# Graph message passing on one core: a round's superblock numbers are loaded into registers once instead of five times

## What is computed

```python
h = jnp.maximum(_layernorm(x, axis=-1), 0.0)
xs = h[src]
for i in range(4):
    msgs = msgs + jnp.where((edge_type == i)[:, None], xs @ W[i] + b[i], 0.0)
out = x + jax.ops.segment_sum(msgs, dst, num_segments=12500)
```

## Time and profile before

| | us |
|---|---|
| median of 3 runs | 2284.09 |
| lowest and highest run | 2275.62, 2289.59 |
| the profiled execution | 2289.54 |
| its span, first to last instruction | 2287.8 |
| POOL busy | 1477.3 (65%) |
| PE busy | 1023.3 (45%) |
| DVE busy | 672.9 (29%) |
| ACT busy | 149.9 (7%) |

### The profile page before, as it was taken

One profiled execution on the slowest core, in us unless ns is written; L12 is line 12 of the kernel. 1 busy time (PEld: TensorE's weight loads), 2 busy tenths in 40 slices (PEclk: granted clock), 3 DMA queues, 4 the chain that ended last, 5 costly groups with the idle time before them and its releaser, 6 DMA issues.

```text
span 2287.8 us, 18293 instructions
## 1 busy us (share of the span) xinstructions
PE 1023.3 (45%) x4086; PEld 704.6 (31%) x4087; DVE 672.9 (29%) x1535; ACT 149.9 (7%) x399; POOL 1477.3 (65%) x1573
## 2 busy tenths in 40 slices
PE   5774243334444444444444444444444444443234
PEld 2232233223232323232323232333233333233234
DVE  5554123133232323232323232323232323121123
ACT  3341000000000000000000000000000000000000
POOL 6666666656666666666666666666666666666663
PEclk9886566666666666666666666666666566655566
DMA  8663111111111111111111111111111111111241
GB/s 249 220 206 111 45 46 44 48 37 45 47 45 47 45 47 45 47 45 47 45 47 45 47 45 47 45 48 45 47 45 46 45 47 45 47 45 45 69 116 43
DMA packets 95392, 144.22 MB, mean 63 GB/s; under 512 B 27481, under 2 KB 57683, under 8 KB 95363
## 3 DMA queue, kind: packets, MB, share of 16 engines
q0 software_dynamic: 50016, 102.50, 17.1%
q1 hardware_dynamic: 40567, 38.92, 5.2%
q10 hardware_dynamic: 4780, 2.51, 0.4%
HBM read 111.73 MB, written 32.09 MB: 63 GB/s over the span
## 4 chain that ended last, share of the span: by engine, by line
POOL 40%; issue 28%; PE 13%; another core or an unknown queue 12%; DVE 3%; DVEq 2%; DMA 1%; ACT 0%; SPq 0%; ACTq 0%; POOLq 0%
POOL messages L367 32%; POOL lists L367 8%; PE ps_sum L815 6%; PE ps_y L773 3%; PE ps_y L839 2%; DVE lists L641 1%; PE ps_y L832 0%; DVE stage L553 0%; PE ps_sum L764 0%; DVEq L661 0%; DVE acc L632 0%; DVE stats L493 0%; DMA lists<-in_dst 0%; DVE ps_node L670 0%
## 5 line engine op out<-in xcount | busy, mean ns | idle before, releaser
L367 POOL DMA_INDIRECT messages<-message_table,table_row x1155 | 1090.0, 944 | 559.5 <-issue 336.1
L815 PE MATMUL ps_sum<-messages,lists 128*128 128x128 f32 x1776 | 353.7, 334 | 440.5 <-issue 407.4
L815 PEld LDWEIGHTS ps_sum<-messages,lists 128*128 128x128 f32 x1776 | 298.3, 238 | 480.9 <-issue 479.3
L632 DVE SCALAR_TENSOR_TENSOR acc<-ps_sum,own_tile,acc x203 | 70.4, 347 | 1112.9 <-remote 1037.6
L367 POOL DMA_INDIRECT lists<-message_table,table_row x288 | 271.8, 944 | 154.2 <-issue 83.0
L815 PE MATMUL ps_sum<-messages,onehot 128*128 128x128 f32 x582 | 132.1, 363 | 274.0 <-issue 256.6
L641 DVE SCALAR_TENSOR_TENSOR lists<-ps_node,node_iota,dst_col 128x1024 f32<-128x1024 f32 x148 | 190.0, 1284 | 114.4 <-issue 55.9
L815 PEld LDWEIGHTS ps_sum<-messages,onehot 128*128 128x128 f32 x582 | 114.8, 269 | 302.3 <-issue 302.2
L815 PE MATMUL ps_sum<-lists 128*128 128x128 f32 x592 | 127.3, 358 | 143.3 <-issue 132.1
L839 PE MATMUL ps_y<-stage 128*128 128x512 f32 x136 | 116.9, 896 | 146.5 <-issue 111.4
L353 POOL DMA_INDIRECT early_x<-in_x,src_col x119 | 112.6, 946 | 65.8 <-issue 33.0
(11 more groups left out here) (89 smaller groups left out, 580.6 us busy)
## 6 DMA issues: line engine op xcount, KB each, us to landing
message_table<-stage SPq DMA_DIRECT2D x98, 256.0 KB
messages<-message_table,table_row POOLq DMA_INDIRECT x1155
out<-acc SPq DMA_DIRECT2D x24, 256.0 KB
lists<-message_table,table_row POOLq DMA_INDIRECT x288
acc<-in_x SPq DMA_DIRECT2D x4, 896.0 KB
early_x<-in_x,src_col POOLq DMA_INDIRECT x119
acc<-in_x ACTq DMA_DIRECT2D x2, 896.0 KB, 5.8
acc<-in_x SPq DMA_DIRECT2D x1, 832.0 KB
```

The lines of the kernel that those rows point to most:

```text
L367: pool.indirect_dma_start(messages[k][0:rows, t, :], None, table_rows, bass.IndirectOffsetOnAxis(ap=flat_rows[0:rows, at + t:at + t + 1], ...
L632: ins = nc.vector.scalar_tensor_tensor(out=rows, in0=sums, scalar=mine[:, bass.ds(place, 1)], in1=rows, op0=ALU.mult, op1=ALU.add)
L815: ins = nc.tensor.matmul(ps_sum[:, bass.ds(q % BANKS, 1), 0:d], onehots[k][:, t, :], messages[k][:, t, :], start=(t == 0), stop=(t == tile ...
```

## The change

VectorE no longer loads its four numbers at each superblock. At the head of a round it loads the 20 numbers of the five superblocks at once into 20 registers, and each superblock copies three of them to the registers it counts with. TensorE gets a row of its own that holds nothing but counts (`windows_row`) and loads the five counts of a round at once into five registers. The early superblocks and the last one keep a load of their own (VectorE with the new function, TensorE's early ones with the old). The new row needs one more VectorE instruction, one more DMA on SP, and all who waited for `ranges_ready` at 16 now wait for 32. POOL's program stays as it is. The diff, cut to its core:

```diff
+    windows_row = sb("windows_row", [1, chunks, sb_per_chunk], I32)
+    windows_by_chunk = sb("windows_by_chunk", [chunks, sb_per_chunk], I32)
...
-            sp.wait_ge(ranges_made, 1)
+            sp.wait_ge(ranges_made, 2)
             sp.dma_start(ranges[:, :, :], ranges_by_chunk[:, :, :].rearrange("c s k -> c (s k)")).then_inc(ranges_ready, 16)
+            sp.dma_start(windows_row[:, :, :], windows_by_chunk[:, :]).then_inc(ranges_ready, 16)
...
             dve.wait_ge(own_steps, 8)
+            nc.vector.tensor_scalar_add(windows_by_chunk[:, :], ranges_by_chunk[:, :, 3], 0.0).then_inc(ranges_made, 1)
...
-            def superblock(s, home, tiles, keys=0):
-                windows_reg = dve.alloc_register(f"dve_windows_{nc.next_id()}")
-                dve.reg_load([at_reg, place_reg, tile_reg, windows_reg], flat_ranges[0:1, bass.ds(s * 4, 4)])
+            def load_round(s, sbs):
+                dve.reg_load([reg for regs in round_regs[0:sbs] for reg in regs], flat_ranges[0:1, bass.ds(s * 4, sbs * 4)])
+
+            def superblock(s, k, home, tiles, keys=0):
+                first_at, first_place, first_tile, windows_reg = round_regs[k]
+                dve.reg_mov(at_reg, first_at)
+                dve.reg_mov(place_reg, first_place)
+                dve.reg_mov(tile_reg, first_tile)
...
                 for m in range(EARLY_ROUNDS * SLOTS):
-                    superblock(s + m, onehots[m % SLOTS], SB_TILES)
+                    if m % SLOTS == 0:
+                        load_round(s + m, SLOTS)
+                    superblock(s + m, m % SLOTS, onehots[m % SLOTS], SB_TILES)
...
-                superblock(i, early_onehot, SB_TILES, keys)
+                load_round(i, 1)
+                superblock(i, 0, early_onehot, SB_TILES, keys)
...
-            def superblock(s, k, tiles, needed, release_slot=True):
-                windows, regs = load_windows(pe, s)
+            def load_round(s, sbs):
+                pe.reg_load(window_regs[0:sbs], flat_windows[0:1, bass.ds(s, sbs)])
+
+            def superblock(k, tiles, needed, release_slot=True):
+                windows = pe.snap(window_regs[k], min_val=1, max_val=node_tiles)
...
             def table_round(i):
+                load_round(i * SLOTS + EARLY_SBS, SLOTS)
                 for k in range(SLOTS):
-                    superblock(EARLY_SBS + i * SLOTS + k, k, SB_TILES, (i + 1) * (16 * SB_TILES))
+                    superblock(k, SB_TILES, (i + 1) * (16 * SB_TILES))
```

More of the change, by code:

```diff
@@ L243, in gnn_program @@
     flat_ranges = ranges[:, :, :].rearrange("p c s -> p (c s)")
+    flat_windows = windows_row[:, :, :].rearrange("p c s -> p (c s)")
     flat_rows = table_row[:, :, :].rearrange("p c t -> p (c t)")
@@ L432, in _ @@
             act.wait_ge(stage_free, 1)
-            act.wait_ge(ranges_ready, 16)
+            act.wait_ge(ranges_ready, 32)
             pair_reg, pair = counter(act, "early_pair")
@@ L591, in _ @@
             dve.wait_ge(own_steps, 10)
-            dve.wait_ge(ranges_ready, 16)
+            dve.wait_ge(ranges_ready, 32)
             for k in range(Y_SLOTS):
@@ L657, in next_pair @@
                 dve.reg_add(pair_reg, pair_reg, 1)
-            def superblock(s, home, tiles, keys=0):
-                windows_reg = dve.alloc_register(f"dve_windows_{nc.next_id()}")
-                dve.reg_load([at_reg, place_reg, tile_reg, windows_reg], flat_ranges[0:1, bass.ds(s * 4, 4)])
+            round_regs = [[dve.alloc_register(f"dve_{name}_{k}") for name in ("at", "place", "tile", "windows")] for k in range(SLOTS)]
+            def load_round(s, sbs):
[5 more added lines that the diff above has]
+                dve.reg_mov(tile_reg, first_tile)
                 windows = dve.snap(windows_reg, min_val=1, max_val=node_tiles)
@@ L750, in _ @@
             table_rounds(rounds - LATE_ROUNDS, rounds)
-            superblock(full_sbs, onehots[0], last_tiles)
+            load_round(full_sbs, 1)
+            superblock(full_sbs, 0, onehots[0], last_tiles)
             settled_windows()
@@ L799, in _ @@
             pe.wait_ge(loaded_b, 16)
-            pe.wait_ge(ranges_ready, 16)
+            pe.wait_ge(ranges_ready, 32)
             pe.wait_ge(y_ready, node_tiles + 2)
@@ L805, in _ @@
             p_reg, early_count = counter(pe, "early_pair")
-            def superblock(s, k, tiles, needed, release_slot=True):
-                windows, regs = load_windows(pe, s)
+            window_regs = [pe.alloc_register(f"pe_windows_{k}") for k in range(SLOTS)]
+            def load_round(s, sbs):
+                pe.reg_load(window_regs[0:sbs], flat_windows[0:1, bass.ds(s, sbs)])
+            def superblock(k, tiles, needed, release_slot=True):
+                windows = pe.snap(window_regs[k], min_val=1, max_val=node_tiles)
                 with pe.Fori(0, windows):
@@ L866, in _ @@
                 table_round(i)
-            superblock(full_sbs, 0, last_tiles, rounds * 16 * SB_TILES + 16 * last_tiles, False)
+            load_round(full_sbs, 1)
+            superblock(0, last_tiles, rounds * 16 * SB_TILES + 16 * last_tiles, False)
 _INS = ["x", "src", "dst", "edge_type_4", "L0_gnn_W", "L0_gnn_b"]
```

6 lines of the change are left out of this document (2 added, 4 removed).

## The result

The change made the kernel slower: median 2354.26 us (2347.84 to 2357.37, four runs) against 2286.84 us for the kernel before (2275.62 to 2304.51, four runs) on the same chip; ratio 1.0284, 95% interval 1.0213 to 1.0355. The profiled execution has a span of 2354.9 us at a granted clock of 0.636, before it was 2287.8.

A forecast was written before the change was run, and what follows sets the result against it. POOL's gathers, 1.420 us each with pauses, were taken as the bound; the parts summed to -0.3 + 0 + 0 + 0 - 1.7 = -2 us, so 2282 us for the median, range 2267 to 2293.

The forecast's parts named there:

- What bounds: POOL's 1443 gathers at 1.420 us, pauses included, take 2049 of 2068 us; some 19 us are waits for others.
- Part 1: 144 loads fewer on TensorE and VectorE each, not on the path in the rounds; 0.3 us gained at the end.
- Part 2: Bigger loads at a round's head, 0.63 us on VectorE and 0.36 on TensorE, hidden: 0, range 0 to +0.9 us.
- Part 3: VectorE's register copies, 69 ns each, replace an address piece of that size: nothing.
- Part 4: Second row's instruction and DMA delay the rounds' start at most 1.1 us, hidden behind the gather: 0, range 0 to +1.
- Part 5: POOL's waits behind early superblocks: marks slightly earlier, three short holes go, 1.7 us gained, of 0 to 30 us.
- Rival B: Mark behind an early superblock misses the quick stretch, POOL stops 17.2 us; two more stops give 2318 us; chance 0.07.
- Rival A: TensorE late by its sequencer in slow stretches; fewer instructions remove all POOL's mark waits, 30 us, giving 2254; chance 0.09.
- C: Count row delays the start, all waiting for two DMAs; 12 us DMA to be seen, 35 for 1%; chance 0.01.
- D: Change doesn't do what it says: a load of 20 at 5 x 344 ns eats the saving, 2284 us, inside the forecast.

The follow-up runs named there:

- h5: Kernel before with both long loads added at each round's head, every short load kept, on a chip with pauses: 2294.54 us, ratio 1.0012.
- e2: Kernel before with VectorE's part alone (one load of twenty per round, register copies), no second row: 2299.39 us, ratio 1.0005.
- e3: Kernel before with only the row of counts and its DMA added, read by nobody, all loads as before: 2300.4 us, ratio 0.9993.
- h1: The change unaltered, repeated on a chip with pauses, against the kernel before: 2370.69 us, ratio 1.0291.
- h2: The change with TensorE's load of five cut into four and one, on a chip with pauses: 2379.72 us, ratio 1.0375 to before.
- e4: The change with both engines' loads cut to at most four registers, on a chip with pauses: 2302.48 us, ratio 1.001 to before.
- f1: The change unaltered on a chip without pauses, against the kernel before: 0.36% faster.
- f5: Kernel before with both long loads added and all short loads kept, on a chip without pauses: the added loads cost nothing.
- g1: The change unaltered, run again on a chip without pauses, against the kernel before: 0.3% faster.
- g5: Kernel before with both long loads added and short ones kept, run again on a chip without pauses: the added loads cost nothing.

## Why the prediction was wrong

The forecast was 2282 us, from 2267 to 2293; 2354.26 were measured.

**What bounds: the count right, the reading wrong.** POOL's gathers do go by 1.42 us each with the pauses. But the prediction took the pauses as given and left 19 us as "POOL's waiting for anybody else". By the signals all 68 waits of the kernel before, 287.1 us, are waits for TensorE's marks. The mark behind the early superblock didn't come 1.2 us ahead of need either: its signal stands at 1286.43, 1.9 us after POOL's gather had ended.

**Part 1, loads taken out: right in count, wrong in "not in the rounds".** 144 loads per engine went. On chips without pauses the time they free is worth nothing to TensorE, and yet the change gains 5.5 to 7.5 us there, by way of POOL (last section, in part argued).

**Part 2, the bigger loads: sizes wrong, and it didn't matter.** I valued 0.63 us for 20 registers and 0.36 for 5. They took 1.35 and 1.24. The first lies inside the upper end of 1.7, the second far above the 0.43 that the same rule gives for five. The slope came from loads of four registers that start at a place in the row divisible by four; TensorE's loads mostly don't, and then even four take 1.01 us. The Trainium skill's 200 ns per register ("Runtime: NRT & Kernel Launch", Instruction fetch mechanics) gives, as an estimate, 1.0 us for five, nearer than mine, and 4.0 for twenty, three times the 1.35 measured. h5 shows that both loads are hidden where the short ones are kept.

**Part 3, the copies.** 240 ns instead of 69, in place of a load of 344 and its piece of 69. All slow runs have them and h5 has not, so whether they play a part in the loss is open; e2, which has them too, lost nothing on its chip.

**Part 4, the second row: right.** Its DMA follows 0.96 us behind the first, TensorE's first matmul still waits 15.10 us for the gather, and e3 is at 0.9993.

```profile
187.30 0.91 SPq L325 DMA_DIRECT2D ranges<-ranges_by_chunk  x1
188.26 0.76 SPq L326 DMA_DIRECT2D windows_row<-windows_by_chunk  x1
...
200.54 3.78 PE L836 MATMUL ps_sum<-messages,onehot 128*128 128x128 f32 x16 [15.10 <-DMA messages<-message_table,table_row]
```

**Part 5, POOL's waits: the step that failed.** I wrote that "the marks behind early superblocks would come earlier by a little" and took 1.7 us of gain. TensorE's work for them did start earlier, at 9 of 13 by 7.2 us after the pause and mostly at 7.1, where the kernel before has 7.9 to 10.7. But an earlier start is no earlier mark: the signal that ScalarE's copy needs missed the quick stretch and came only when POOL had run its next burst and stopped, 10 us and more behind the matmul. I treated the slow stretches as a cost per instruction, in which fewer instructions can only help; the signals of TensorE keep a timetable there, in which leaving sooner can mean the later train. That the mark's signal was late at 9 early superblocks, and what it cost, is shown; that the earlier start is the reason is argued.

**Rival B: right in place and kind, rated 0.07.** It named the miss of the quick stretch through "a shift of the slow stretch against POOL's holes". Against it I had set that nothing gets longer there than the load, by 0.06 us. It was 0.94 us (1.24 against 0.30), and getting shorter shifts as well. Its size was off: a wait costs 10 us, not 17.2, and the pauses shrink in return (43.1 us in all), so each late copy costs some 7 us; nine came, in h1 and h2 eleven and twelve, where I priced two.

**Rival A** had the idea that the sequencer's instructions count in the slow stretches. Loads went, and the waits rose by 101.1 us instead of going. **C and D** didn't come.

## What to carry over

Where an engine far behind the bound is released in bursts, don't value work taken from it at "nothing or a gain": look in the trace at how far each of its hand-overs lies from the edge of the burst, and give a loss a real chance when the margin is 1 to 3 us. Before blaming an added instruction, add it without removing anything, as h5 does; that one run ruled out that the loads do it alone. Measure what a cut run really cuts: TensorE's load in pieces was longer than the whole. When a view names nobody for a wait, look up the semaphore before taking the wait as given. And run the change itself as a control in every job, since two chips can differ by more (15%) than the change (3%).

## What the runs showed of the hardware that I had not expected

**Two kinds of chip.** The same kernel before takes 2287 to 2302 us in four comparisons and 1980 to 1985 in three. In the traces of the latter POOL never pauses, a gather starts each 1.25 us throughout, and the 16 key matmuls take 6.5 us from first start to last instead of 26. On chips with pauses, slow matmuls start in steps of 0.70 us (1.41, 2.11 and 2.80 apart at 1054 to 1070), and so do the lengths of POOL's pauses: 0.8, 2.2, 2.9, 3.6, 4.4. What hands out these steps, and holds TensorE's signals back until POOL pauses, no trace names, and all runs here were recorded. The Trainium skill, "NOTIFIC — the notification-queue block", section 7.1, says that the block that writes the recorder's notices can hold back the engines; no run here shows whether it does.

**What a load costs goes by its place.** Medians, from the change, e4, h2 and h5, and the same in the traces without pauses:

```
registers   first place divisible by four   any other place
1           0.30 us                         0.30 us
4           0.34                            1.01
5           0.59                            1.24
20          1.35                            -
```

TensorE's loads of a round start at places 15, 20, 25 and so on in their row, so one in four is of the quick kind. VectorE's loads start at multiples of four throughout. A further group of up to four registers costs 0.25 us at a divisible place; elsewhere it is some 0.23 us for each further register. By this, a row of counts with eight places per round would give TensorE the quick kind each time; that was not tried.

**Why the change gains 0.3% without pauses.** There POOL's pace is all: busy 1479.0 us in f1 against 1488.6 in f5. In f5, 30 of 1443 gathers take over 1.0 us, 8.0 us of excess over 944 ns in all; in f1 only 8 do, 2.0 us. In g1 and g5 it is 8 and 27 gathers, 1.7 and 6.6 us, yet POOL's busy time differs by 1.9 us alone there (1482.3 against 1484.2). Of the longest, nearly all begin 0.08 to 0.21 us after VectorE's key places (line 685) and end 0.8 us after they do. VectorE and POOL of f5, then of f1, where both start together and the gather takes 0.94:

```profile
436.55 0.75 DVE L685 SCALAR_TENSOR_TENSOR ps_i<-node_iota,key_iota 128x512 f32<-128x512 f32 x1
...
436.64 1.47 POOL L371 DMA_INDIRECT messages<-message_table,table_row  x1 [0.30 <-issue]
```

```profile
635.98 0.75 DVE L685 SCALAR_TENSOR_TENSOR ps_i<-node_iota,key_iota 128x512 f32<-128x512 f32 x1
...
635.98 0.94 POOL L371 DMA_INDIRECT messages<-message_table,table_row  x1 [0.30 <-issue]
```

In the change VectorE's instruction and the gather start together here; that the load of 0.34 us taken from the superblock's head is what shifts them is argued. The Trainium skill ("SBUF — State Buffer", section Who interferes with whom) says that a VectorE instruction with two inputs in SBUF locks out a GpSimd one that reads SBUF until it is done. Line 685 has two such inputs, and the trace agrees: the gather started at 436.64 ends at 438.11, and one that starts with the instruction isn't held. That the stretched gathers are the whole 5.5 to 7.5 us is not shown: between f5 and f1 their excess differs by 6.0 us and the profiled executions by 9.4, between g5 and g1 by 4.9 and 1.7.
